# One transformer layer on one core: who places low parts and weights in the first chunk, and the last rows stored in blocks of 128 tokens

## The chip, the cores and the metric

The kernel runs on 1 core of one Trainium2 chip. The metric is the device time of one execution in microseconds (us). The kernel before took 2363.05 us, the median of 3 runs (2362.56 to 2366.21).

## What is computed

The reference is one layer: a layer norm of the input, an attention block and a feed-forward block that both read the normed input, and their sum added to the input. Cut to what matters:

```
xn = layernorm(x)                                  # x: 2 x 1024 x 1024, float32
q, k, v = bitnet(xn, Wq), bitnet(xn, Wk), bitnet(xn, Wv)   # 32 query heads, 8 key/value heads of 32
attn = softmax(q k^T / sqrt(32)) v
x + bitnet(attn, Wo) + ffn(xn)                     # ffn: gate and up 1024 -> 3584, down 3584 -> 1024, 4-bit weights

bitnet(x, W): s = max(mean(|W|, axis=1), 1e-8)
              y = (x @ sign(W)^T) * (s * scale)    # nan_to_num afterwards
```

So a projection needs two things of every weight tile: its signs, turned so that the input channel lies on the partitions, and the mean of its magnitudes, one number for each output channel.

## The kernel before

All 2048 tokens are taken in four chunks of 512 (`c` from 0 to 3), a chunk being four tiles of 128 tokens (`i`). The program goes: normalise and project the four chunks to q, k and v; attention over 32 units, with the first score rows woven into the last projections; the output projection; the feed-forward block over two halves of the tokens, gate and up first, then down; at the end of each half the sums are turned back to token rows and stored. There is no scheduler: every engine runs a list written out by hand, in order, and waits on named semaphores.

What happens ahead of the first projection and in chunk 0 (lines are those of the profile):

- VectorE takes the moments of the four first x tiles (L953, L954), normalises them (L987, L991), and ScalarE writes the float16 high part of each tile (`high`, L708). VectorE writes the low part, the remainder (`low`, L997). TensorE turns both, eight 128x128 transposes a tile (`turn_high` L1392, `turn_low` L1400). High parts go to PSUM bank 6 (tiles 0, 2) or 2 (tiles 1, 3), low parts to the bank after it, so a bank must be emptied before the tile after next can be turned. ScalarE copies both into `xT` (`evac_high` L678, `evac_low` L683).
- Twelve weight tiles of 128x1024 are loaded by SyncE's queue (L341) into eight places; tiles 8 to 11 wait until place 0 to 3 has been read for its signs and its magnitudes. For each tile ScalarE takes the signs (`signs`, L690, two buffers), TensorE turns them (`turn_weights`, L1384, PSUM banks 4 and 5), and somebody copies the result into `wT`: VectorE for the odd tiles from 3 on (`place_weights`, L1015), ScalarE for the others (`evac_weights`, L696). VectorE reduces each tile to its magnitudes (`magnitude`, L948). After all twelve it works out the channel scales `cc` (`cm_ok` is counted up when they stand), GpSimd takes a maximum over partitions (L591), and VectorE works out the three factors `fac` (`fac_ok`, L1055).
- TensorE's chunk is twelve projections of 16 matmuls 128x512 (`project`, L1439), p from 0 to 11, the two value tiles first. Between those of chunk 0 it turns the weights that later ones need: tiles 2 and 3 after p = 0, 4 and 5 after p = 1, 6 and 7 after p = 2, 8 after p = 3, 9 after p = 4, 10 after p = 6, 11 after p = 8. After p = 4 it turns the two value outputs (`turn_values`, L1453), and from p = 6 on it turns the x tiles of the next chunk; the first of these, `turn_high(4)`, writes bank 6 and so waits until the turned values there have been copied.
- Each projection is emptied and scaled by ScalarE (`evac_output`, L746, counts `y_ok`), which also writes a mask (`mask_output`, L753, one buffer); VectorE clamps and mends the output (`guard_output`, L1077 and L1081, counts `r_ok`), ScalarE writes its float16 head (L759) and VectorE its tail (L1094). Between these VectorE takes moments and normalises the next chunk, and in chunk 0 it places the turned values (`place_values`, L1087). The outputs of p = 0 to 3 stand in banks 0 to 3; p = 4 writes bank 0 again and so needs `y_ok` of p = 0.

At the end of the program, for the second half of the tokens, the last visits of `pe_down` (L1655) are scaled by ScalarE (L922) and VectorE (L1347), in two pairs of bank groups (`s2` 0: banks 0 to 3, `s2` 1: banks 4 to 7). Then `pe_turn` (L1671) turns four groups of 4 x 4 blocks, VectorE adds the input rows (`dve_turn`, L1355, 16 instructions of 128x512), and SyncE stores each group with one transfer of 1 MB (`store_rows`, L504). The first turn waits until every visit has been scaled.

```
            for k in (2, 4):
                evac_weights(k)
                signs(k + 2)
                signs(k + 3)
...
            act.wait_ge(s["fac_ok"], 1)
            for c in range(NC):
```

This is ScalarE's list just ahead of its first `evac_output`: the wait for the factors stands in front of all outputs, and tiles 6 and up are placed behind the first of them.

## Time and profile before

| what | value |
|---|---|
| median of the runs | 2363.05 us |
| the profiled execution's own time | 2364.19 us |
| its span, first to last instruction | 2362.1 us |
| TensorE busy (matmul) | 2305.1 us, 98% of the span |
| VectorE, ScalarE, GpSimd busy | 76%, 67%, 41% |
| TensorE's mean granted clock | 0.995 of full |

Busy time counts an engine's compute instructions alone. The span is cut in the page into 40 slices; TensorE is at 9 tenths or more in all of them but the first (6 tenths) and the last (8 tenths). The chain of work that ended last is TensorE's from about 1089 us on, broken by a few pieces of VectorE, and VectorE's at the very end.

### The profile page before, as it was taken

The page shows a single profiled execution, that of the slowest core. Times are in us where ns is not written, and L with a number is a line of the kernel's source. Part 1 is how long each engine was busy: PE and PEld are TensorE (multiplying, and loading weights), DVE is VectorE, ACT ScalarE, POOL GpSimd, SP SyncE. Part 2 cuts the span into 40 slices and gives each one's busy share as a digit, 9 for nine tenths or more (in the row PEclk, how much of TensorE's full clock was granted, in tenths as well). Part 3 has the DMA queues.
Part 4 walks back from the last instruction along what each step waited for, and adds up shares of the span by engine and source line. Part 5 has one row for each costly group of instructions (what it writes and reads, how often), then busy time and mean ns, then how long its engine had stood idle before and what let it go on. Part 6 is the DMA issues. An engine that isn't in the chain of part 4 may idle for free.

```text
span 2362.1 us, 45029 instructions
## 1 busy us (share of the span) xinstructions
PE 2305.1 (98%) x18561; PEld 1020.5 (43%) x18561; DVE 1802.5 (76%) x2314; ACT 1581.5 (67%) x2050; POOL 967.6 (41%) x531
## 2 busy tenths in 40 slices
PE   6999999999999999999999999999999999999998
PEld 3443344444444444434444444444444444444444
DVE  7878888888888888846577777777777777777777
ACT  5774788888888888872266666666665666666664
POOL 0000599999999999980022222210002222221000
PEclk9999999999999999999999999999999999999999
DMA  5130466555666655663211111131124111114111
GB/s 184 36 100 5 82 92 97 90 92 89 91 90 99 91 90 90 88 116 112 90 36 36 36 36 36 52 110 36 36 72 143 36 36 36 36 50 182 36 36 72
DMA packets 179905, 175.52 MB, mean 74 GB/s; under 512 B 87586, under 2 KB 127394, under 8 KB 179702
## 3 DMA queue, kind: packets, MB, share of 16 engines
q1 hardware_dynamic: 117430, 150.62, 20.5%
q0 software_dynamic: 62272, 22.03, 12.3%
q8 instruction: 147, 2.41, 0.4%
q14 instruction: 56, 0.46, 0.1%
HBM read 160.08 MB, written 65.45 MB: 95 GB/s over the span
## 4 chain that ended last, share of the span: by engine, by line
PE 53%; DVE 1%; issue 0%; ACT 0%; DVEq 0%
PE ps L1639 33%; PE ps L1655 16%; PE ps L1610 4%; PE ps L1671 0%; DVE zone L1355 0%; DVE xT L1355 0%; PE ps L1523 0%; DVE sm L1248 0%; ACT zone L922 0%; DVE zone L1065 0%; DVE zone L1066 0%; DVE zone L1259 0%; DVEq L140 0%; ACT zone L862 0%; DVE zone L1069 0%
## 5 line engine op out<-in xcount | busy, mean ns | idle before, releaser
L1639 PE MATMUL ps<-xT,zone 128*128 128x512 f16 x3584 | 774.6, 379 | 2.7 <-DVE zone L1355 2.7
L1103 DVE TENSOR_REDUCE zone<-ps 128x1 f32<-128x512 f32 x1024 | 639.2, 683 | 142.0 <-PE ps L1414 138.1
L779 ACT ACTIVATE zone<-ps,sm 128x512 f32<-128x512 f32 x1024 | 623.9, 698 | 144.8 <-PE ps L1464 144.2
L605 POOL TENSOR_TENSOR zone<-zone 128x1024 f32<-128x1024 f32 x252 | 643.9, 2687 | 135.8 <-ACT zone L779 102.8
L1332 DVE TENSOR_SCALAR ps<-ps,zone_c 128x1024 f32<-128x1024 f32 x392 | 506.7, 1293 | 160.8 <-PE ps L1639 158.7
L903 ACT ACTIVATE ps<-ps,zone_c 128x1024 f32<-128x1024 f32 x392 | 426.6, 1088 | 259.9 <-PE ps L1639 259.9
L1639 PEld LDWEIGHTS ps<-xT,zone 128*128 128x128 f16 x3584 | 350.2, 98 | 426.3 <-DVE zone L1355 4.2
L1464 PE MATMUL ps<-zone 98*32 98x512 f16 x4096 | 408.4, 380 | 4.2 <-ACT zone L779 3.8
L1414 PE MATMUL ps<-zone 96*32 96x512 f16 x4096 | 407.5, 381 | 4.5 <-issue 2.5
L1655 PE MATMUL ps<-zone 128*128 128x512 f16 x1792 | 387.1, 379 | 0.0
L1343 DVE TENSOR_SCALAR ps<-ps,zone_c 128x1024 f32<-128x1024 f32 x216 | 279.2, 1293 | 93.1 <-PE ps L1655 92.9
L651 POOL CAST zone<-zone 128x1024 f16<-128x1024 f32 x56 | 58.1, 1037 | 703.5 <-DVE zone L1336 703.5
L917 ACT ACTIVATE ps<-ps,zone_c 128x1024 f32<-128x1024 f32 x216 | 235.1, 1088 | 137.8 <-PE ps L1655 137.8
L1478 PE MATMUL ps<-zone 128*32 128x512 f32 x2048 | 268.6, 595 | 2.6 <-ACT zone L779 0.7
L1655 PEld LDWEIGHTS ps<-zone 128*128 128x128 f16 x1792 | 175.4, 98 | 211.4
L1464 PEld LDWEIGHTS ps<-zone 98*32 98x32 f16 x4096 | 117.7, 96 | 180.4 <-ACT zone L779 80.8
L1414 PEld LDWEIGHTS ps<-zone 96*32 96x32 f16 x4096 | 115.3, 96 | 180.1 <-DVE zone L1103 76.9
L1439 PE MATMUL ps<-xT,zone 128*128 128x512 f16 x768 | 180.3, 390 | 3.0 <-ACT xT L683 3.0
L659 POOL TENSOR_TENSOR xT<-xT,zone 128x1024 f32<-128x1024 f32 x8 | 18.7, 2355 | 361.8 <-ACT zone L922 361.8
L1493 PE MATMUL ps<-zone 128*32 128x512 f32 x1024 | 133.2, 592 | 0.4 <-DVE zone_c L1114 0.4
L653 POOL TENSOR_TENSOR zone<-zone 128x1024 f16<-128x1024 f32 x56 | 119.1, 2127 | 4.5
L1439 PEld LDWEIGHTS ps<-xT,zone 128*128 128x128 f16 x768 | 74.1, 100 | 97.7 <-issue 21.5
(137 smaller groups left out, 1331.5 us busy)
## 6 DMA issues: line engine op xcount, KB each, us to landing
zone<-dequantised SPq DMA_DIRECT2D x84, 512.0 KB, 3.6
dequantised<-zero_points SPq DMA_DIRECT2D x84, 256.0 KB, 4.3
zone<-zone SPq DMA_DIRECT2D x384, 32.0 KB, 2.4
zone<-_attn_hidden_states_dram SPq DMA_DIRECT2D x16, 512.0 KB, 6.4
zone<-inverse_sums SPq DMA_DIRECT2D x128, 64.0 KB, 2.5
attention<-zone SPq DMA_DIRECT2D x32, 256.0 KB, 2.0
xT<-attention SPq DMA_DIRECT2D x4, 2048.0 KB, 12.0
dequantised<-in_L_ffn_gate_w_dram POOLq DMA_DIRECT2D x28, 256.0 KB, 6.3
```

The costliest lines, as they stand in the source:

```text
L605: nc.gpsimd.tensor_tensor(duo[n % 3], prob[:, prob_slot(e), :], prob[:, prob_slot(e + 2), :], add).then_inc(s["sum_ok"], 1)
L779: A(prob[:, prob_slot(e), m % 2 * 512:(m % 2 + 1) * 512], ps[:, 3 + m % 3, :], ACT.Exp, scale=gam[:, 0:1]).then_inc(s["exp_ok"], 1)
L903: A(pair, pair, ACT.Copy, scale=tab[:, t, 0, g:g + 1]).then_inc(s["act_ok"], 1)
L1103: V.tensor_reduce(mxs[:, u % 2, half, i % 16:i % 16 + 1], ps[:, (2 * i + half) % 3, :], AX, amax).then_inc(s["max_ok"], 1)
L1332: V.tensor_scalar(pair, pair, tab[:, t, 1, g:g + 1], None, mult).then_inc(s["dve_ok"], 1)
L1343: V.tensor_scalar(pair, pair, dtab[:, it, o:o + 1], None, mult).then_inc(s["dve_ok"], 1)
L1414: last = MM(ps[32 * a:32 * a + 32, c % 3, :], qst[u % 3][0:96, i % 16 // 4, c0:c0 + 32], kst[0:96, u // 2 % 2, half * 512:(half + 1) * 512 ...
L1439: last = MM(ps[:, output_bank(n), :], wT[:, kt, f * P:(f + 1) * P], xT[:, b2, part, kt, s2 * 512:(s2 + 1) * 512], start=(kt == 0 and part ...
L1464: last = MM(ps[32 * b:32 * b + 32, 3 + m % 3, :], kst[0:98, u // 2 % 2, kt * P + 32 * b:kt * P + 32 * b + 32], qst[u % 3][0:98, 2 * hp + a ...
L1478: last = MM(ps[32 * h:32 * h + 32, 6, :], vst[:, u // 2 % 2, kt, :], prob[:, prob_slot(2 * kt + h // 2), h % 2 * 512:(h % 2 + 1) * 512], s ...
L1639: last = MM(ps[:, 4 * s2 + 2 * m + c, :], ring[:, buf, m * H + g * P:m * H + (g + 1) * P], xT[:, hf, part, g, c * 512:(c + 1) * 512], star ...
L1655: last = MM(ps[:, 4 * s2 + 2 * m + c, :], ring[:, k % RING, (it % 4) * 512 + o * P:(it % 4) * 512 + (o + 1) * P], hT[:, it, part, c * 512: ...
```

## The change

Four parts.

1. Low parts. VectorE copies the low parts of tiles 0, 1 and 3 of chunk 0 out of PSUM (`place_low`), two of them before and after its own `low(3)`; ScalarE keeps that of tile 2. The waits follow through a new semaphore, `xlv_out`.
2. Weights and magnitudes. VectorE reduces all twelve weight tiles in one run. ScalarE places tiles 2 to 6 (VectorE keeps 7, 9, 11), each behind the signs of the tile two further on, and takes the signs of tiles 8 and 9 ahead of its first `evac_output`. That output now waits for `cm_ok` in place of `fac_ok`.
3. First values. The turned values of chunk 0 are placed by ScalarE like those of the other chunks (`evac_turned_values(0)`, at p = 4), and `place_values` goes. On ScalarE `high(4)` moves from p = 4 to p = 3 and `high(5)` from p = 5 to p = 4.
4. Last rows. Each of the last four groups is stored by four transfers of 256 KB, one for each VectorE instruction, and the first of the last turns no longer waits for the very last visit.

```diff
@@ wait_weights and by_dve
-            return k % 2 == 1 and k >= 3
+            return k % 2 == 1 and k >= 7
@@ new, on PE in turn_low, project and turn_values
+        def wait_low_parts(engine, n):
+            engine.wait_ge(s["xlv_out"], min(n, 2) if n < 4 else 3)
+            if n >= 3:
+                engine.wait_ge(s["xl_out"], 1 if n < 5 else n - 3)
@@ SyncE
+            def store_blocks(n):
+                for b in range(4):
+                    sp.wait_ge(s["turn_ok"], 4 * (4 + n) + b + 1)
+                    sp.dma_start(rows_of(out, 1, n)[:, b, :], rows(1, n)[:, b, :]).then_inc(s["out_ok"], 16)
...
-                store_rows(1, n)
-            sp.wait_ge(s["out_ok"], 16 * 8)
+                store_blocks(n)
+            sp.wait_ge(s["out_ok"], 16 * (4 + 16))
@@ ScalarE, ahead of the outputs
             evac_high(1)
             high(3)
-            evac_low(0)
-            evac_low(1)
             evac_high(2)
+            evac_high(3)
             evac_low(2)
-            evac_high(3)
-            evac_low(3)
             signs(2)
             signs(3)
-            for k in (2, 4):
+            for k in range(2, 7):
+                signs(k + 2)
                 evac_weights(k)
-                signs(k + 2)
-                signs(k + 3)
+            signs(9)
...
-            act.wait_ge(s["fac_ok"], 1)
+            act.wait_ge(s["cm_ok"], 1)
@@ ScalarE, chunk 0
-                        if p == 0:
-                            evac_weights(6)
-                            signs(8)
-                            signs(9)
-                        elif p == 3:
+                        if p == 3:
                             evac_weights(8)
                             signs(10)
                         elif p == 4:
                             signs(11)
+                            act.wait_ge(s["fac_ok"], 1)
+                            evac_turned_values(0)
                         elif p == 7:
                             evac_weights(10)
                     mask_output(c, p)
+                    if c == 0 and p == 3:
+                        act.wait_ge(s["fac_ok"], 1)
+                        high(i)
...
-                            high(i)
-                        elif p == 5:
+                            high(i if c else i + 1)
+                        elif p == 5 and c:
                             high(i + 1)
@@ VectorE
-            for i in range(4):
+            for i in range(3):
                 low(i)
-            for k in range(3):
+            place_low(0)
+            low(3)
+            place_low(1)
+            place_low(3)
+            for k in range(NW):
                 magnitude(k)
...
-            for k in range(3, 5):
-                magnitude(k)
-            place_weights(3)
-            for k in range(5, 8):
-                magnitude(k)
-            place_weights(5)
-            for k in range(8, 12):
-                magnitude(k)
...
-                    if c == 0 and p == 4:
-                        place_values()
@@ PE
-                            pe.wait_ge(s["v_out" if c else "v0_out"], 2 * c if c else 2)
+                            pe.wait_ge(s["v_out"], 2 * c + 2)
...
-                pe_turn(1, n, n % 2, HALVES * HALF_VISITS)
+                pe_turn(1, n, n % 2, HALVES * HALF_VISITS - (n == 0))
```

VectorE's list from the low parts to the magnitudes. Before (the first rows are `low` on tiles 0, 1 and on 2, 3; TENSOR_REDUCE is `magnitude`; COPY is `place_weights(3)` and `(5)`):

```order
L997 SCALAR_TENSOR_TENSOR zone<-zone,sm 128x1024 [waits h_ok] x2
L997 SCALAR_TENSOR_TENSOR zone<-zone,sm 128x1024 [waits xl_pe,h_ok] x2
L948 TENSOR_REDUCE sm<-zone 128x1 [waits w_in0]
...
L948 TENSOR_REDUCE sm<-zone 128x1 [waits w_in4]
L1015 COPY zone<-ps 128x8x128 [waits wT_pe]
L948 TENSOR_REDUCE sm<-zone 128x1 [waits w_in5]
```

And with the change (COPY to `xT` is `place_low`, of tile 0, then of tiles 1 and 3):

```order
L1006 SCALAR_TENSOR_TENSOR zone<-zone,sm 128x1024 [waits h_ok] x2
L1006 SCALAR_TENSOR_TENSOR zone<-zone,sm 128x1024 [waits xl_pe,h_ok]
L1018 COPY xT<-ps 128x8x128 [waits xl_pe]
L1006 SCALAR_TENSOR_TENSOR zone<-zone,sm 128x1024 [waits xl_pe,h_ok]
L1018 COPY xT<-ps 128x8x128 [waits xl_pe] x2
L957 TENSOR_REDUCE sm<-zone 128x1 [waits w_in0]
L957 TENSOR_REDUCE sm<-zone 128x1 [waits w_in1]
```

Three copies came in ahead of the magnitudes, and the two copies of weight tiles that stood among them are gone.

ScalarE's list around the first output. Before (zone<-zone 128x1024 is `signs`, zone<-ps 128x8x128 is `evac_weights`, zone<-ps,sm 128x512 is `evac_output`):

```order
L690 ACTIVATE zone<-zone 128x1024 [waits wT_pe,w_in6]
L690 ACTIVATE zone<-zone 128x1024 [waits wT_pe,w_in7]
L746 ACTIVATE zone<-ps,sm 128x512 [waits qkv_pe,fac_ok]
L696 ACTIVATE zone<-ps 128x8x128 [waits wT_pe]
L690 ACTIVATE zone<-zone 128x1024 [waits wT_pe,w_in0]
L690 ACTIVATE zone<-zone 128x1024 [waits wT_pe,w_in1]
L753 ACTIVATE zone_c<-zone 128x512 [waits y_ok]
```

And with the change:

```order
L701 ACTIVATE zone<-zone 128x1024 [waits wT_pe,w_in7]
L707 ACTIVATE zone<-ps 128x8x128 [waits wT_pe]
L701 ACTIVATE zone<-zone 128x1024 [waits wT_pe,w_in0]
L707 ACTIVATE zone<-ps 128x8x128 [waits wT_pe]
L701 ACTIVATE zone<-zone 128x1024 [waits wT_pe,w_in1]
L754 ACTIVATE zone<-ps,sm 128x512 [waits qkv_pe,cm_ok]
L761 ACTIVATE zone_c<-zone 128x512 [waits y_ok]
```

The first output stood ahead of weight tile 6 and of the signs of tiles 8 and 9, and stands behind them now.

## Rows read from the trace of the kernel before

**Rows 1.** The page, busy time of each engine over the span.

```profile
PE 2305.1 (98%) x18561; PEld 1020.5 (43%) x18561; DVE 1802.5 (76%) x2314; ACT 1581.5 (67%) x2050; POOL 967.6 (41%) x531
```

**Rows 2.** Timeline of TensorE, start and duration in us, with idle and releaser.

```profile
25.38 0.61 PE L1400 MATMUL ps<-id,zone 128*128 128x128 f16 x8 [0.31 <-ACT xT L683]
29.04 6.14 PE L1439 MATMUL ps<-xT,zone 128*128 128x512 f16 x16 [3.05 <-ACT xT L683]
...
35.91 3.62 PE L1439 MATMUL ps<-xT,zone 128*128 128x512 f16 x16
...
44.60 3.62 PE L1439 MATMUL ps<-xT,zone 128*128 128x512 f16 x16
50.76 0.62 PE L1384 MATMUL ps<-id,zone 128*128 128x128 f16 x8 [2.54 <-ACT zone L690]
51.21 5.30 PE L1439 MATMUL ps<-xT,zone 128*128 128x512 f16 x16
...
58.15 7.07 PE L1439 MATMUL ps<-xT,zone 128*128 128x512 f16 x32
...
69.43 1.04 PE L1392 MATMUL ps<-id,zone 128*128 128x128 f16 x8 [3.76 <-DVE zone L1087]
70.26 6.04 PE L1439 MATMUL ps<-xT,zone 128*128 128x512 f16 x16
```

**Rows 3.** Busy time by stretch: PE, PEld, DVE, ACT, POOL; then clock, DMA, GB/s.

```profile
29.00:36.00 7.00, 6.96 (x33) 3.17 (x34) 1.43 (x2) 2.12 (x3) 0.00 (x0) 0.63 0.87 264
...
66.00:77.00 11.00, 7.57 (x40) 3.92 (x41) 10.32 (x16) 9.56 (x14) 0.00 (x0) 0.69 0.60 191
77.00:108.00 31.00, 31.00 (x186) 15.85 (x184) 22.62 (x46) 22.14 (x33) 0.00 (x0) 1.00 0.01 1
```

**Rows 4.** Timeline of VectorE, 23 to 63 us.

```profile
23.51 1.28 DVE L997 SCALAR_TENSOR_TENSOR zone<-zone,sm 128x1024 f16<-128x1024 f32 x1 [0.73 <-PE ps L1400]
...
24.71 5.72 DVE L948 TENSOR_REDUCE sm<-zone 128x1 f32<-128x1024 f32 x5
...
45.76 0.17 DVE L1031 TENSOR_SCALAR sm<-sm 128x12 f32<-128x12 f32 x1
...
48.03 0.68 DVE L1015 COPY zone<-ps 128x1024 f16<-128x1024 f16 x1
...
52.25 0.75 DVE L1081 COPY_PREDICATED zone<-zone_c,zone 128x512 f32<-128x512 int32 x1 [0.84 <-ACT zone_c L753]
...
56.84 0.77 DVE L1081 COPY_PREDICATED zone<-zone_c,zone 128x512 f32<-128x512 int32 x1
...
61.69 0.73 DVE L1081 COPY_PREDICATED zone<-zone_c,zone 128x512 f32<-128x512 int32 x1
```

**Rows 5.** Groups of ScalarE by line and shape, 29 to 90 us: busy, mean ns; idle.

```profile
L690 ACT ACTIVATE zone<-zone 128x1024 f16<-128x1024 f32 x10 | 10.1, 1060 | 0.0
L746 ACT ACTIVATE zone<-ps,sm 128x512 f32<-128x512 f32 x11 | 7.5, 680 | 6.7 <-DVE sm L1055 5.2 <-PE ps L1439 1.5
...
L696 ACT ACTIVATE zone<-ps 128x1024 f16<-128x1024 f16 x5 | 5.1, 1019 | 6.3 <-PE ps L1384 6.3
```

**Rows 6.** Timeline of the end, all engines.

```profile
2344.34 1.28 DVE L1347 SCALAR_TENSOR_TENSOR xT<-ps,zone_c,xT 128x1024 f32<-128x1024 f32 x1 [0.44 <-PE ps L1655]
...
2345.72 5.54 PE L1671 MATMUL ps<-id,xT 128*128 128x128 f32 x48 [1.42 <-issue]
2346.46 10.62 DVE L1355 SCALAR_TENSOR_TENSOR xT<-ps,sm,xT 128x512 f32<-128x512 f32 x16 [0.84 <-PE ps L1671]
2349.21 8.27 SPq L504 DMA_DIRECT2D out_dram<-xT  x4
```

**Rows 7.** Source of the row stores L504: time from issue to landing.

```profile
DMA to landing us min/median/max: 4.2/4.3/4.5
```

**Rows 8.** Source of the 256 KB attention stores L489: time from issue to landing.

```profile
DMA to landing us min/median/max: 2.0/2.0/5.2
```

**Rows 9.** DMA queues, 2349 to 2362 us: GB/s in 40 slices.

```profile
GB/s 0 0 0 208 365 391 391 391 384 365 372 321 403 391 384 403 384 372 359 328 397 410 365 397 397 365 391 321 397 391 391 378 397 359 384 397 378 177 0 0
```

35 lines of the change are left out of this document (18 added, 17 removed).

## The prediction, made before the change was run

> **What bounds the kernel now.** I read the page first. TensorE is busy 98% of the span [rows 1], so a change pays only where TensorE stands still, where it runs at the lower clock, or behind its last matmul. The page's slices put both places at the two ends, and the change touches just these. Next comes TensorE's own timeline of chunk 0 [rows 2]. The reader is to see three stalls with their releasers: 3.05 us ahead of the first projection (ScalarE's low parts), 2.54 us ahead of weight tile 8 (ScalarE's signs), 3.76 us ahead of `turn_high(4)` (VectorE's `place_values`). Behind each stall the next 16 matmuls take 6.14, 5.30 and 6.04 us, where the undisturbed ones take 3.62. The stretches show why: the granted clock is 0.63 in 29 to 36 us and 0.69 in 66 to 77 us, so part of each ran at the lower of the two levels, 1.2 GHz, and from 77 us on TensorE is full at clock 1.00 [rows 3]. So chunk 0 is the last place where the other engines hold it up for long. Then I read the lists of VectorE and ScalarE in that stretch [rows 4, 5] for what they do while TensorE waits, and the end of the timeline with the DMA views [rows 6 to 9].
>
> Consecutive instructions overlap by about 0.1 us on both engines: five magnitudes fill 5.72 us [rows 4], a step of 1.13. By the same overlap a sign costs ScalarE about 0.95, a weight copy 0.91, an output 0.6 [rows 5].
>
> **Part 1, low parts.** Before, ScalarE copied all eight tiles, the last of them just ahead of 29.04. Now VectorE ends `low(3)` at 24.79 as before (23.51 + 1.28) [rows 4], places tile 1 by 25.4 (a copy of this shape takes 0.68 [rows 4]), TensorE turns the low part of tile 3 at 25.5 where it did at 25.38 (0.61 [rows 2]), and VectorE places that by 26.8. ScalarE's share behind its last `high` is three copies where it was six, 2.7 us less, so it is no longer last. The first projection starts at 26.9, not 29.04: **2.1 us**. What is queued behind the new copies is the run of magnitudes, costed next. The stall is shorter and the matmuls are dense earlier, so the clock should rise earlier within the projection: I take 5.1 us for it where it took 6.14, **1.0 us** (bounds: 0, and 2.5 where it runs as the undisturbed one of 3.62). Sum 3.1: the second projection starts at 32.8, not 35.91 [rows 2].
>
> **Part 2, weights and magnitudes.** The next three projections go at 4.35 us each, turns of weights included (35.91 to 44.60 in two [rows 2]). Ahead of the first output ScalarE owes two signs and two copies in such a period, 2 x 0.95 + 2 x 0.91 = 3.7 us, so it keeps up, and the fourth projection ends at 32.8 + 2 x 4.35 + 3.6 = 45.1. VectorE's magnitudes start at 26.7, and 12 x 1.13 brings them to 40.3. Before they ended at 45.7, when the scales began [rows 4]. So `cm_ok` stands at 41.6. ScalarE is through with the signs of tile 9 at about 44.1, so the first output is there at 44.8. TensorE wants it at 45.4, for the fifth projection. So the stall of 2.54 goes, and so does the slow stretch behind it: the fifth projection starts at 45.4, not 51.21, and takes 3.6, not 5.30. **Gain so far 7.3.** The cover here is thin, 0.6 us; if ScalarE is later by more, TensorE waits for it one to one.
>
> What is late next: the second value output must have passed VectorE before `turn_values` ends. VectorE needs 9.6 us from `place_weights(7)` to there (48.03 to 57.61 [rows 4]), of which 0.84 waited for a mask that ScalarE now writes earlier. From the factors at 42.6 that is 51.2. TensorE is there at 49.7: a wait of 1.5 where there was nearly none. The sixth projection starts at 51.7, not 58.15: gain 6.4.
>
> **Part 3, first values.** Two projections and one turn take 7.4 us (58.15 to 65.67 [rows 2]): TensorE is at `turn_high(4)` at 59.1. ScalarE now empties the values behind: the third output through VectorE at 55.9 (4.8 after the second, as 57.61 to 62.42 [rows 4]), then a mask 0.5, `high(4)` 1.0, a head 0.6, an output 0.7, signs 0.95, and the two copies 1.25: 61.0. TensorE waits 2.0 instead of 3.76 and resumes at 61.1, not 69.43: gain 8.3. A slow stretch may follow (6.04 before; I take 4.9). VectorE's `low(4)` is through at about 67.7, one microsecond behind TensorE, and two copies of high parts are 0.4 late each. I take 0.8 to 1.9 off for these: **the head gives 7.5** when TensorE's full stretch is reached. After that the same work follows, full, and nothing there is tied to absolute time. The three loads of SyncE that now wait for later magnitudes (weight tiles 9 to 11, one for each 1.13 us) are read 8 us after their issue and cost nothing. Bounds: 4.5, if the clock gives nothing back and ScalarE is 1 us late, and 9.
>
> The Trainium skill (TensorE: Matmul & The Clock Gate, the part on the clock gate) says that the number of slow matmuls at a start varies between runs of one kernel. One profile can't show that; it is a reason to expect some scatter.
>
> **Part 4, last rows.** The first turn waited for VectorE's last scaling (to 2345.62) and now comes right behind the last matmul, at 2344.3. Its transposes are done before VectorE is free, so VectorE starts its 16 adds at 2345.6, not 2346.46 [rows 6]: 0.84. They fill 10.62 without a gap and end at 2356.2. The stores: four of 1 MB at intervals of 2.64 us, each landing after 4.3 [rows 6, 7], the last at 2361.6; the pipe moves the 4.19 MB (16 x 256 KB) at some 385 GB/s all the time [rows 9], 10.9 us. Now the first 256 KB leaves at 2346.4 in place of 2349.21. By the pipe the end is 2346.4 + 0.9 (before it moved data 0.9 after the issue) + 10.9 = 2358.2. By the last add it is 2356.2 + 2.0, for the nearest row of that size, the attention stores [rows 8], = 2358.2. **3.1 us**, taking 0.3 off because both limits meet. Bounds: 0.8, if smaller transfers move slower by as much as they start earlier, and 3.6.
>
> The attention stores of 256 KB land in 2.0 us in the trace [rows 8]. The Trainium skill (DMA: Bandwidth & Descriptors, Anatomy of one DMA) gives about 2.0 us fixed plus the bytes at 436 GB/s, by a fit for the other path of issue, and its rules for kernel authors ask for 1 MiB or more in one DMA. By its sum the last store would land 2.6 us after its add, and part 4 would give 2.5.
>
> **Sum.** 7.5 + 3.1 = 10.6 us against the profiled execution's own 2364.19: 2353.6 us. That execution is 1.1 us above the median of the runs. Three slow stretches make up 6.6 us of its chunk 0, so a median run may have had one less; the changed kernel has fewer of them to lose, and I keep 2353.6.
>
> **Rivals.**
>
> *The helpers become the bound in chunk 0.* For it: VectorE is busy 10.32 of 11 us and ScalarE 9.56 in 66 to 77 [rows 3], and the change moves two value copies and two weight copies onto ScalarE. Then the waits after p = 4 grow and the clock falls again: the head gives about 4, the time is 2364.2 - 4 - 3.1 = 2357. Against it: ScalarE idles 6.7 us ahead of its outputs and 6.3 ahead of weight copies [rows 5], nearly all before 48.2 us, and there it gets most of its new work.
>
> *The stores gain nothing but the earlier adds,* since the pipe is full already [rows 9] and each transfer adds a little: 2364.2 - 7.5 - 0.8 = 2355.9.
>
> *What chunk 0 gives is lost later,* in waits of the attention stage that were covered: 2361. Against it, TensorE is full for 31 us behind chunk 0 [rows 3] and 98% over all [rows 1].
>
> *Slower: the queue runs one store at a time.* If each 256 KB store held SyncE's queue for its 2.0 us [rows 8], 16 would take 32 us from 2346.4 and end at 2378.4, 16.8 later than now; less the head's 7.5, the time would be 2373.5. It decides from about 1.4 us a store. By the page's sum of 2.6 us each it would be 41.6 us. Against it: four stores land after 4.3 each and are issued 2.64 apart [rows 6, 7], so two are in flight together, and the rate never drops between them.
>
> **How the numbers follow.** Forecast 0.74, helpers 0.12, stores 0.06, lost later 0.05, one at a time 0.03. The range takes in the first three and the bounds of the clock's part: 2350.5 to 2358.2. A measurement of this kernel can tell some 0.2% from no change, 4.7 us, so faster means below 2358.3. Faster: all of the first and third case and most of the second, 0.90. Same: the fourth and the rest, 0.07. Slower: 0.03.
>
> **What would show it.** First projection at about 26.9; no stall ahead of weight tile 8 and no slow stretch in the fifth projection; stalls of about 1.5 at the second `turn_values` (released by VectorE) and 2 at `turn_high(4)` (by ScalarE's value copies); the second chunk's first projection 7 to 8 us earlier; 16 stores 0.66 apart, the last landing about 2 us after the last add. Wrong if the first output comes after TensorE wants it, if the clock stays at 1.2 GHz through the fifth projection, or if the last store lands over 4 us after its add.

## The result, and the profile after

| | median of the runs | lowest to highest | ratio to the kernel before (95% interval) |
|---|---|---|---|
| changed kernel, first comparison | 2353.12 us (5 runs) | 2351.58 to 2358.72 | 0.9957 (0.9944 to 0.9971) |
| changed kernel, second comparison (e9 below) | 2355.84 us (8 runs) | 2353.08 to 2358.99 | 0.9974 (0.9964 to 0.9984) |

The kernel before took 2366.21 us in the first comparison (5 runs) and 2361.94 us in the second (13 runs). The ratio is not taken from the two medians, so it need not be their quotient. As time the ratios are gains of 10.1 us (6.9 to 13.3) and 6.1 us (3.8 to 8.5). The predicted 2353.6 us is met; the predicted gain of 10.6 us lies within the first interval and above the second. The stages below tell what of it the change earned. A stage is a stretch of TensorE's own timeline: the head up to the last projection of chunk 0, the middle, and the end behind the last matmul of `pe_down`.

The profiled execution of the changed kernel took 2351.58 us, span 2349.7, against 2364.19 and 2362.1 before. Where the 12.4 us between the two spans lie:

| stage | before | after | gain | predicted |
|---|---|---|---|---|
| head: to the start of the last projection of chunk 0 | 90.15 | 83.26 | 6.9 | 7.5 |
| middle: from there to the end of the last matmul of `pe_down` | 2254.1 | 2250.8 | 3.4 | 0 |
| end: from there to the end of the span | 17.8 | 15.7 | 2.1 | 3.1 |

Of the page's busy times [rows 1] only TensorE's moved, by 7.5 us; 6.6 us of that are the three slow stretches of chunk 0, which are gone:

```profile
PE 2297.6 (98%) x18561; PEld 1019.1 (43%) x18561; DVE 1802.8 (77%) x2313; ACT 1581.5 (67%) x2051; POOL 966.9 (41%) x531
```

TensorE's timeline of chunk 0 in the changed kernel, to be laid beside [rows 2] (L1439 is a projection, L1384 `turn_weights`, L1456 `turn_values`, L1392 `turn_high`, L1400 `turn_low`):

```profile
27.28 3.61 PE L1439 MATMUL ps<-xT,zone 128*128 128x512 f16 x16 [0.99 <-DVE xT L1018]
...
31.62 3.62 PE L1439 MATMUL ps<-xT,zone 128*128 128x512 f16 x16
...
44.22 3.62 PE L1439 MATMUL ps<-xT,zone 128*128 128x512 f16 x16
...
51.80 0.66 PE L1456 MATMUL ps<-id,zone 128*128 128x128 f32 x4 [3.08 <-DVE zone L1090]
52.29 7.07 PE L1439 MATMUL ps<-xT,zone 128*128 128x512 f16 x32
...
61.63 0.62 PE L1392 MATMUL ps<-id,zone 128*128 128x128 f16 x8 [1.82 <-ACT zone L774]
62.09 3.62 PE L1439 MATMUL ps<-xT,zone 128*128 128x512 f16 x16
...
68.34 0.62 PE L1400 MATMUL ps<-id,zone 128*128 128x128 f16 x8 [2.64 <-DVE zone L1006]
...
83.26 15.92 PE L1439 MATMUL ps<-xT,zone 128*128 128x512 f16 x73
```

The first projection starts 1.76 us earlier and takes 3.61 us where it took 6.14, so the second starts 4.3 earlier. The stall of 2.54 ahead of weight tile 8 is gone, and the fifth projection starts at 44.22 instead of 51.21: 7.0 us ahead. The lead is 5.9 us at the sixth projection, 8.2 at the eighth (62.09 for 70.26) and 6.9 at the last one of chunk 0, so behind the fifth nothing is won that lasts. Three stalls follow, 3.08, 1.82 and 2.64 us, in place of the one of 3.76. The same stretches as in [rows 3] show the clock (columns: stretch, length, then PE, PEld, DVE, ACT, POOL busy; granted clock, DMA share, GB/s):

```profile
29.00:36.00 7.00, 7.00 (x58) 4.17 (x57) 7.00 (x8) 4.05 (x5) 0.00 (x0) 1.00 0.88 296
...
66.00:72.00 6.00, 3.65 (x29) 2.18 (x30) 5.74 (x9) 5.91 (x9) 0.00 (x0) 1.00 0.44 145
```

The granted clock is 1.00, 2.4 GHz, in both. Between 66 and 72 us TensorE has work for 3.65 us of the 6, while VectorE is busy 5.74 and ScalarE 5.91: the helpers hold it up. VectorE's timeline, beside [rows 4], shows why the stall of 3.08 exists: the magnitudes are one run of 13.60 us from 26.94 on, and the mended outputs (COPY_PREDICATED) end at 51.75 and 56.59.

```profile
26.94 13.60 DVE L957 TENSOR_REDUCE sm<-zone 128x1 f32<-128x1024 f32 x12
...
51.02 0.73 DVE L1090 COPY_PREDICATED zone<-zone_c,zone 128x512 f32<-128x512 int32 x1
...
55.84 0.75 DVE L1090 COPY_PREDICATED zone<-zone_c,zone 128x512 f32<-128x512 int32 x1
...
67.01 1.27 DVE L1006 SCALAR_TENSOR_TENSOR zone<-zone,sm 128x1024 f16<-128x1024 f32 x1
```

The end, all engines, beside [rows 6]:

```profile
2333.86 3.66 PE L1674 MATMUL ps<-id,xT 128*128 128x128 f32 x32
2334.07 1.28 DVE L1347 SCALAR_TENSOR_TENSOR xT<-ps,zone_c,xT 128x1024 f32<-128x1024 f32 x1 [0.44 <-PE ps L1658]
2335.27 10.62 DVE L1355 SCALAR_TENSOR_TENSOR xT<-ps,sm,xT 128x512 f32<-128x512 f32 x16
...
2336.04 10.45 SPq L515 DMA_DIRECT2D out_dram<-xT  x16
```

The turn starts with the end of the last matmul and VectorE adds without the wait of 0.84, as predicted. The source of the new stores L515 (16 of 256 KB; duration of the issue in ns) and, in the next line, their landing (the time from the issue until the store is reported complete), beside [rows 7]:

```profile
L515 SPq DMA_DIRECT2D out_dram<-xT x16: 332/416/855, 2336.0 to 2345.9; - x16
...
DMA to landing us min/median/max: 2.4/2.8/3.5
```

The last store is issued at 2345.9 with the last add and lands 3.4 us later, not 2.0. The DMA queues from 2334 to 2350 us, GB/s in 40 slices, beside [rows 9]:

```profile
GB/s 0 0 0 0 0 41 0 276 338 31 312 389 394 364 389 389 379 374 379 389 374 404 364 384 394 364 389 369 379 394 364 384 379 399 374 358 31 0 0 0
```

The start has a hole (31 between 338 and 312). VectorE isn't its cause: the second store was issued as soon as its add was done, at 2336.70, but the issue took 855 ns. Another transfer lies there, which the view of these queues lists as `q8 instruction`, 16 KB: it began at 2336.30 (the slice with 41) and took 0.9 us of one of the 16 DMA engines. From the twelfth slice on the pipe is as full as before, and it is last. The section on the stores comes back to this transfer.

### The profile page after: what moved, and what is told of

The parts are those of the page before. It is cut to its first block, busy times and chain, and to the rows that moved or that the text cites. A ratio compares the mean times of both kernels' runs of the same rounds, so it can differ in the third digit from the quotient of the medians.

```text
span 2349.7 us, 45046 instructions
## 1 busy us (share of the span) xinstructions
PE 2297.6 (98%) x18561; PEld 1019.1 (43%) x18561; DVE 1802.8 (77%) x2313; ACT 1581.5 (67%) x2051; POOL 966.9 (41%) x531
## 4 chain that ended last, share of the span: by engine, by line
PE 90%; DVE 5%; ACT 3%; issue 1%; DMA 0%; SPq 0%; POOL 0%; DVEq 0%; ACTq 0%
PE ps L1642 33%; PE ps L1658 16%; PE ps L1414 10%; PE ps L1467 9%; PE ps L1481 9%; PE ps L1496 5%; PE ps L1613 4%; PE ps L1439 3%; DVE sm L957 1%; ACT zone L787 1%; ACT zone L719 0%; DVE zone L996 0%; ACT zone L767 0%; DVE zone L1090 0%; ACT zone L754 0%
## 5 line engine op out<-in xcount | busy, mean ns | idle before, releaser
L1642 PEld LDWEIGHTS ps<-xT,zone 128*128 128x128 f16 x3584 | 350.3, 98 | 426.2 <-DVE zone L1355 4.2
L1658 PE MATMUL ps<-zone 128*128 128x512 f16 x1792 | 387.1, 379 | 0.0
L1439 PE MATMUL ps<-xT,zone 128*128 128x512 f16 x768 | 173.7, 379 | 1.0 <-DVE xT L1018 1.0
L670 POOL TENSOR_TENSOR xT<-xT,zone 128x1024 f32<-128x1024 f32 x8 | 18.7, 2362 | 361.8 <-ACT zone L931 361.8
L1613 PE MATMUL ps<-zone 128*128 128x512 f16 x512 | 112.3, 379 | 1.2 <-DVE zone L1259 1.1
```

The costliest lines, as they stand in the source:

```text
L1642: last = MM(ps[:, 4 * s2 + 2 * m + c, :], ring[:, buf, m * H + g * P:m * H + (g + 1) * P], xT[:, hf, part, g, c * 512:(c + 1) * 512], star ...
L1658: last = MM(ps[:, 4 * s2 + 2 * m + c, :], ring[:, k % RING, (it % 4) * 512 + o * P:(it % 4) * 512 + (o + 1) * P], hT[:, it, part, c * 512: ...
```

## The experiments

Twelve kernels ran, each with profiled and timed runs beside the kernel before. One table for all; the start of the second chunk, of which the expectations speak, is 3.45 us behind the last projection of chunk 0 in every trace.

| kernel | first projection | last projection of chunk 0 | last matmul of `pe_down` ends | end stage | median (runs) | ratio (95%) |
|---|---|---|---|---|---|---|
| before | 29.04 | 90.15 | 2344.30 | 17.8 | | |
| changed | 27.28 | 83.26 | 2334.03 | 15.7 | 2353.12 (5) | 0.9957 (0.9944 to 0.9971) |
| e9 changed again | 27.29 | 83.94 | 2338.39 | 16.3 | 2355.84 (8) | 0.9974 (0.9964 to 0.9984) |
| e1 end only | 28.80 | 87.89 | 2341.68 | 15.9 | 2360.23 (10) | 0.9993 (0.9983 to 1.0003) |
| e2 head only | 27.25 | 83.74 | 2336.01 | 17.8 | 2356.87 (7) | 0.9975 (0.9964 to 0.9985) |
| e5 part 1 undone | 28.97 | 86.27 | 2346.31 | 16.1 | 2357.80 (10) | 0.9979 (0.9968 to 0.9990) |
| e6 part 3 undone | 26.79 | 82.73 | 2336.48 | 16.3 | 2355.21 (5) | 0.9968 (0.9955 to 0.9981) |
| e7 output ahead of weights | 27.21 | 83.86 | 2345.06 | 15.7 | 2357.76 (10) | 0.9983 (0.9973 to 0.9993) |
| e3 stores of 1 MB | 27.26 | 83.19 | 2334.78 | 16.8 | 2355.73 (7) | 0.9969 (0.9958 to 0.9981) |
| e4 1 MB x3, then 256 KB x4 | 27.25 | 83.17 | 2335.08 | 17.9 | 2355.79 (6) | 0.9969 (0.9958 to 0.9981) |
| e10 stores of 512 KB | 28.53 | 84.47 | 2337.59 | 16.4 | 2355.45 (6) | 0.9967 (0.9955 to 0.9979) |
| e8 values, low(4) earlier | 28.57 | 83.52 | 2335.01 | 15.9 | 2352.44 (4) | 0.9959 (0.9944 to 0.9974) |
| e11 no mask in chunk 0 | 27.76 | 77.24 | 2335.89 | 15.8 | 2351.99 (4) | 0.9951 (0.9937 to 0.9965) |
| e12 mask by GpSimd | 27.04 | 88.80 | 2343.29 | 15.7 | 2361.84 (12) | 0.9998 (0.9986 to 1.0009) |

The kernel before had a median of 2361.89 us (23 runs) beside e1, e2, e5 and e6, 2362.50 (18) beside e7, e3, e4 and e8, 2361.94 (13) beside e9, e10 and e11, and 2362.33 (17) beside e12.

### The end alone, and the head alone (e1, e2)

e1 is the kernel before with part 4; e2 is the changed kernel without it:

```diff
# e2, against the changed kernel
-                store_blocks(n)
-            sp.wait_ge(s["out_ok"], 16 * (4 + 16))
+                store_rows(1, n)
+            sp.wait_ge(s["out_ok"], 16 * 8)
...
-                pe_turn(1, n, n % 2, HALVES * HALF_VISITS - (n == 0))
+                pe_turn(1, n, n % 2, HALVES * HALF_VISITS)
```

> The kernel before with part 4 alone. My theory: the stage behind the last matmul shrinks as in the changed kernel, from 17.8 us (last down matmul to the end of the span) to 15.7, and nothing else moves: the second chunk's first projection stays at 91 to 94 us, and the time is 2.1 us below before. Rival (the small stores owe their gain to the clock or to chance of that run): 17 or more, time within 1 us of before.

> The changed kernel with part 4 undone (1 MB stores, first turn behind the last visit). My theory: the second chunk's first projection at 86.1 to 87.1 us as in the changed kernel, the end stage 17.8 us, the time 7 to 10 us below before and about 2 above the changed kernel. Rival (the head's gain is not its own but comes of one execution without slow stretches of the clock): the time within 5 us of before.

e1: the end stage went from 17.8 to 15.9 us, and the median from 2361.89 to 2360.23, 1.7 less, with an interval that takes in no change. e2: 5.0 us less in the median, 3.5 to 8.5 by the ratio, for 7 to 10 expected. The two medians add up to 6.7 us, the two ratios to 7.6, each with some 2.4 us either way. What TensorE's timeline of e1, whose head is the old one, shows:

```profile
28.80 5.27 PE L1445 MATMUL ps<-xT,zone 128*128 128x512 f16 x16 [2.96 <-ACT xT L689]
...
49.65 1.03 PE L1390 MATMUL ps<-id,zone 128*128 128x128 f16 x8 [2.53 <-ACT zone L696]
50.47 4.71 PE L1445 MATMUL ps<-xT,zone 128*128 128x512 f16 x16
...
68.26 0.62 PE L1398 MATMUL ps<-id,zone 128*128 128x128 f16 x8 [3.76 <-DVE zone L1093]
68.72 3.62 PE L1445 MATMUL ps<-xT,zone 128*128 128x512 f16 x16
```

The stalls are those of [rows 2] to a tenth, but the clock is kinder: 5.27, 4.71 and 3.62 us for the three projections that took 6.14, 5.30 and 6.04. The three are 3.9 us shorter together and the first starts 0.2 earlier, yet the last projection of chunk 0 comes only 2.3 earlier (87.89 for 90.15): TensorE then waits for VectorE and ScalarE in places where it didn't before (0.23, 0.31 and 0.26 us). So the old head takes 87.9 or 90.2 us, mostly by the clock. The new one takes 82.7 to 84.5 over seven traces of it (changed, e9, e2, e3, e4, e10) or with part 3 undone (e6). The head is worth 4 to 7 us (3.4 where e10's inputs came late), according to which two executions are compared.

### Part 1: low parts back to ScalarE (e5)

```diff
             evac_high(1)
             high(3)
+            evac_low(0)
+            evac_low(1)
             evac_high(2)
-            evac_high(3)
             evac_low(2)
+            evac_high(3)
+            evac_low(3)
@@ VectorE
-            for i in range(3):
+            for i in range(4):
                 low(i)
-            place_low(0)
-            low(3)
-            place_low(1)
-            place_low(3)
```

> Part 1 undone in the changed kernel: ScalarE copies all eight tiles of chunk 0 again. My theory: the first projection starts at 29.0 instead of 27.3 us, with a slow stretch behind it (the first projection takes 5 to 6 us), and the second chunk starts at 87.6 to 88.7 instead of 86.7; time 1 to 3 us above the changed kernel. Rival (VectorE and ScalarE, by their whole work in chunk 0, set when the second chunk starts, and the first projection's start does not matter): 86.7 to 87.2, the same time.

TensorE's timeline of e5:

```profile
28.97 6.28 PE L1436 MATMUL ps<-xT,zone 128*128 128x512 f16 x16 [3.05 <-ACT xT L692]
...
54.10 0.66 PE L1453 MATMUL ps<-id,zone 128*128 128x128 f32 x4 [1.01 <-DVE zone L1087]
...
70.64 0.62 PE L1397 MATMUL ps<-id,zone 128*128 128x128 f16 x8 [2.63 <-DVE zone L1007]
```

The old stall of 3.05 is back, with a slow projection of 6.28 us behind it, and the last projection of chunk 0 starts at 86.27, 3.0 later (expected for the second chunk: 87.6 to 88.7; measured 89.7). The second projection is 4.4 us late, but the stall at `turn_values` is 1.01 instead of 3.08, and behind it TensorE is 2.3 late: almost half of the delay is absorbed by a stall in which TensorE would have waited for VectorE anyway. The further 0.7 is a slow stretch at the ninth projection, which e9 has with the whole change.

The second `turn_values` also tells what the parts are worth there. It starts at 51.80 in the changed kernel, 54.10 with part 1 undone, 56.50 in e1 and 57.66 before. So part 1 is worth 2.3 us at that point, and part 2 another 2.4 (against e1) to 3.6 (against before). Of part 2 only the order around the first output was undone by itself (e7); that the run of magnitudes, freed of the two weight copies, makes up the rest is not shown by a run.

### Part 3: first values back to VectorE (e6)

```diff
@@ ScalarE
                         elif p == 4:
                             signs(11)
-                            act.wait_ge(s["fac_ok"], 1)
-                            evac_turned_values(0)
...
-                            high(i if c else i + 1)
+                            high(i)
@@ VectorE
+                    if c == 0 and p == 4:
+                        place_values()
```

> Part 3 undone in the changed kernel: VectorE places the first values, high(4) and high(5) back in their old places. By the stall alone (my prediction's way of counting) TensorE resumes at turn_high(4) 2 us later, the eighth projection (p = 7) starts at about 64 instead of 62.1, and all behind it is 2 us later: second chunk at 88.7, time 2 us above the changed kernel. Rival (the helpers' total work bounds chunk 0): the stall at turn_high(4) grows by 2 us, but the later one of 2.6 us at turn_low(4) shrinks by as much, and the second chunk starts at 86.5 to 87.3, the same time.

TensorE's timeline of e6:

```profile
51.31 0.65 PE L1463 MATMUL ps<-id,zone 128*128 128x128 f32 x4 [1.39 <-DVE zone L1088]
...
63.09 0.62 PE L1399 MATMUL ps<-id,zone 128*128 128x128 f16 x8 [3.77 <-DVE zone L1094]
63.55 5.30 PE L1446 MATMUL ps<-xT,zone 128*128 128x512 f16 x16
```

The stall at `turn_high(4)` is 3.77 us again, as before the change, instead of 1.82; it even brings a slow projection of 5.30. But the stall at `turn_low(4)`, 2.64 in the changed kernel, is gone, and the last projection of chunk 0 starts at 82.73, half a microsecond *earlier* than with part 3. Moving the value copies to ScalarE moved the wait from one place to the next; the head gained nothing by it. (Its first projection was itself 0.5 us earlier: from first to last projection both take 56.0 us to within 0.1, so it is a tie.)

### Half of part 2: the first output ahead of tile 6 (e7)

```diff
-            for k in range(2, 7):
+            for k in range(2, 6):
                 signs(k + 2)
                 evac_weights(k)
-            signs(9)
...
-            act.wait_ge(s["cm_ok"], 1)
+            act.wait_ge(s["fac_ok"], 1)
...
-                        if p == 3:
+                        if p == 0:
+                            evac_weights(6)
+                            signs(8)
+                            signs(9)
+                        elif p == 3:
```

> Half of part 2 undone in the changed kernel: ScalarE's first output waits for the factors again and stands ahead of weight tile 6 and of the signs of tiles 8 and 9. My theory: TensorE waits about 2 us for the signs of tile 8 ahead of the fifth projection (start 46 to 46.5 instead of 44.2), the wait of 3.1 at the second turned values shrinks to 2, and the second chunk starts at 87.0 to 87.7 instead of 86.7: time 0.5 to 1.5 above the changed kernel. Rival (one to one): 88.7 and 2 us.

TensorE's timeline of e7:

```profile
45.57 0.62 PE L1387 MATMUL ps<-id,zone 128*128 128x128 f16 x8 [1.71 <-ACT zone L701]
...
52.42 0.66 PE L1459 MATMUL ps<-id,zone 128*128 128x128 f32 x4 [1.88 <-DVE zone L1093]
```

A stall of 1.71 for ScalarE's signs is back, the fifth projection starts 1.8 later, and the stall at `turn_values` shrinks from 3.08 to 1.88. The last projection of chunk 0 starts at 83.86 (so the second chunk at 87.3; 87.0 to 87.7 expected), inside what two executions of the changed kernel gave (83.26 and 83.94). Against the first of them, which like e7 has no slow projection, the order around the first output is worth 0.6 us. e7's median is higher than its head explains; its profiled execution lost time in the middle, told below.

### The stores: 1 MB, 512 KB, and small ones behind large ones (e3, e10, e4)

```diff
# e3: stores of 1 MB, the early first turn kept
-                store_blocks(n)
-            sp.wait_ge(s["out_ok"], 16 * (4 + 16))
+                store_rows(1, n)
+            sp.wait_ge(s["out_ok"], 16 * 8)
# e10: pairs of blocks
-                for b in range(4):
-                    sp.wait_ge(s["turn_ok"], 4 * (4 + n) + b + 1)
-                    sp.dma_start(rows_of(out, 1, n)[:, b, :], ...
+                for b in (0, 2):
+                    sp.wait_ge(s["turn_ok"], 4 * (4 + n) + b + 2)
+                    sp.dma_start(rows_of(out, 1, n)[:, b:b + 2, :], ...
# e4: only the last group in blocks
-            for n in range(4):
-                store_blocks(n)
+            for n in range(3):
+                store_rows(1, n)
+            store_blocks(3)
```

> The changed kernel with 1 MB stores: of part 4 only the earlier first turn is left. If each store lands 4.3 us after its issue, the end stage is 0.9 shorter than before: 16.8 us, with the last add 3.9 to 5 ahead of the end as before; time 1.1 above the changed kernel. If the pipe's rate set the end, the same 16.8 would come out, but the landings would be over 4.5.

> The changed kernel with the last rows stored by 512 KB (eight stores). By the pipe's rate with its holes: with 1 MB stores all data took 11.2 us from the first packet to the last, with 256 KB 12.0 to 12.7, with holes near the start. Halves start 0.66 us later than quarters, and if holes come with the number of transfers the data takes about 11.4: end stage 15.6 to 15.9 us, the same as or a little below the quarters. Rival (the landing of the last store sets it: 3.0 to 3.3 for 512 KB behind the last add instead of 2.8): 16.2 or more.

> The changed kernel with three stores of 1 MB and only the fourth group in four of 256 KB. If the landing time of the last small store sets the end (2.0 us by the prediction's row), the end stage is 15.7 us or less, as with 16 small ones. If the pipe's rate does (385 GB/s from the first store on), it has started 2 us later and ends later: 16.2 to 16.8 us.

e3's end stage is 16.8 us, as expected: the early turn gives 0.9, and smaller stores the rest, down to 15.7 to 16.3 over the nine traces that have all of part 4. e10 took 16.4, not the 15.6 to 15.9 expected. e4 took 17.9, all that the early turn had given and more; neither theory expected it (15.7, or 16.2 to 16.8). Its four small stores L515 at the source, the landing of its three 1 MB stores L509, and its DMA queues from 2338 to 2353 us:

```profile
L515 SPq DMA_DIRECT2D out_dram<-xT x4: 539/1187/1213, 2345.0 to 2348.1; - x4
...
DMA to landing us min/median/max: 4.9/5.8/6.0
```

```profile
GB/s 0 0 0 0 0 317 344 377 355 377 360 371 339 399 393 399 366 388 360 371 371 426 366 410 366 366 415 361 404 382 366 415 361 404 224 27 27 22 0 0
```

The issues of the small stores took 1187 ns in the median, where they took 416 in the changed kernel, so the last one left SyncE at 2349.3, some 2.4 us behind the last add. The last slices, 27, 27 and 22 GB/s where the full pipe has some 385, are about what one of the 16 engines moves (24): one has packets left when the others are through.

It is tempting to blame the mixture of small stores with large ones, but the first 1 MB store already landed 6.0 us behind its issue, at 2345.05, where e3's took 4.3; the first small store was issued only at 2344.99. What differs before that is the transfer `q8 instruction` met above. In e4 it began at 2340.1, inside the first store (DMA queues, 2339 to 2342 us), and 3.2% of 16 engines over 3 us are 1.5 us of one engine:

```profile
q8 instruction: 1, 0.02, 3.2%
```

In the traces of before, e2 and e3 it came ahead of the first store. In e10 it began at 2342.6, inside the second store, and took 1.4 us of one engine; the tail is of the same kind (35, 23 and 18 GB/s in the last slices from 2340 to 2354 us). The small stores show the same. e6, where it began at 2344.3, has the landings of its stores before it (source L516, issued from 2338 to 2342.5 us) and from it on (2344 to 2350):

```profile
DMA to landing us min/median/max: 2.0/2.1/2.2
...
DMA to landing us min/median/max: 2.6/3.1/3.9
```

One issue of 1146 ns stands right behind it; the nine traces with all of part 4 each have one such issue of 0.9 to 1.3 us there. Where the transfer came within 1 us of the first store the end stage was 15.7 to 16.1 us (seven traces), where it came in the middle of the row 16.3 (e9, e6). Without the last 1.3 us, in which few engines had packets, e4 would be at 16.7, within the 16.2 to 16.8 of the pipe's rate. So the 17.9 of e4 and the 16.4 of e10 are no verdict on mixed sizes or on 512 KB: like against like, e10's 16.4 stands beside 16.3 with 256 KB. All this is read from one trace of each kernel; no run moved the transfer by itself, and why the issues of small stores behind large ones stayed at 1.2 us isn't shown.

From first to last packet the 4.19 MB took 11.2 us in 1 MB stores (before, e2, e3) and 12.0 to 12.7 in stores of 256 KB (changed 12.0, e9 12.7). Full, the pipe takes 0.70 us for 256 KB and VectorE makes them in 0.66, so small stores have no slack in which a delayed engine could catch up.

### Who bounds chunk 0 now (e8, e11, e12)

e8 is the changed kernel with the value copies of ScalarE at p = 3 instead of 4 (and the signs of tile 11 behind them), and VectorE's `low(4)` at p = 5 instead of 6. e11 leaves out mask and mending of the twelve outputs of chunk 0, the work of `nan_to_num`; VectorE clamps the output in place and nothing else. e12 is e8 with the masks of chunk 0 made by GpSimd.

```diff
# e8
-                        elif p == 4:
-                            signs(11)
                             act.wait_ge(s["fac_ok"], 1)
                             evac_turned_values(0)
+                        elif p == 4:
+                            signs(11)
@@ VectorE
+                        if (c, p) == (0, 5):
+                            low(i)
# e11 and e12, ScalarE
-                    mask_output(c, p)
+                    if c:
+                        mask_output(c, p)
# e12, GpSimd
+            for p in range(12):
+                pool.wait_ge(s["y_ok"], p + 1)
+                if p >= 1:
+                    pool.wait_ge(s["r_ok"], p)
+                nc.gpsimd.tensor_tensor(mask, output(p), output(p), sub).then_inc(s["mask_ok"], 1)
```

> The changed kernel with two things moved in chunk 0: ScalarE places the first values at p = 3, ahead of the mask that waits for VectorE, and VectorE writes low(4) at p = 5 instead of p = 6. My theory: the stall at turn_high(4) (1.8 us) goes, the one at turn_low(4) (2.6 us) shrinks to under 1, but the helpers' work holds the second chunk: start at 85.2 to 85.9 instead of 86.7, time about 1 below the changed kernel. Rival (each stall counts in full): 83 and 3.5 us below.

> The changed kernel, in chunk 0 without the mask and the mending of the projections' outputs (ScalarE's mask_output and VectorE's predicated copy are left out, the clamp writes the output): the guard against values that aren't numbers is missing in that chunk. This takes 0.53 us x 12 from ScalarE and 0.63 us x 12 from VectorE. If the helpers' work bounds chunk 0, the second chunk's first projection starts at 79.5 to 81 us instead of 86.7, and the waits of TensorE behind the fifth projection shrink from 7.8 us to 3. Rival (the waits come of the order of the lists, not of the load): less than 3 us earlier, over 83.5.

> e8's order (first values and low(4) earlier) and, in chunk 0, the mask written by GpSimd as output minus output, so that ScalarE has 0.53 us x 12 less to do; nothing is left out. From the first projection's start to the second chunk's it was 59.4 to 60.1 us in five executions of the changed kernel's order or near it, 58.3 in e8, and 52.9 without mask and mending. If the helpers' load bounds chunk 0: 56.5 to 57.5, and the time 1.5 to 3 us below the changed kernel, 8 to 10 below before. Rival (GpSimd's instruction of 1.3 to 1.6 us comes too late for VectorE's mending, or slows VectorE): 58.5 or more, no gain over e8.

TensorE's timelines of e8 and of e11:

```profile
53.09 1.09 PE L1458 MATMUL ps<-id,zone 128*128 128x128 f32 x4 [3.08 <-DVE zone L1090]
...
68.93 0.61 PE L1394 MATMUL ps<-id,zone 128*128 128x128 f16 x8 [1.80 <-ACT xT L689]
```

```profile
50.56 0.66 PE L1460 MATMUL ps<-id,zone 128*128 128x128 f32 x4 [1.36 <-DVE zone L1088]
...
63.27 0.62 PE L1404 MATMUL ps<-id,zone 128*128 128x128 f16 x8 [0.80 <-DVE zone L1007]
...
77.24 17.43 PE L1443 MATMUL ps<-xT,zone 128*128 128x512 f16 x80
```

e11: with one instruction of ScalarE and one of VectorE less for each output, the stalls shrink to 1.36 and 0.80 and the last projection starts at 77.24, so the second chunk at 80.7 (expected 79.5 to 81). From first to last projection that is 49.5 us instead of 56.0. So the work of VectorE and ScalarE on the outputs bounds chunk 0 after the change. Leaving it out takes load off both and also shortens the way of each output, which e11 can't tell apart; the busy times of the changed kernel speak for the load. From 26.9 to 61.5 us VectorE works 32.8 of 34.6 us, and then, up to the last projection, it is ScalarE that is busy 20.43 of 21.30 (columns as above):

```profile
62.00:83.30 21.30, 18.09 (x134) 9.91 (x132) 16.20 (x23) 20.43 (x29) 0.00 (x0) 1.00 0.30 99
```

Not all of e11's 6.5 us reaches the time: its median is 3.9 us below e9's, measured beside it, and its middle took 2258.7 us, 4.2 more than e9's. One profile of each can't say whether that is the scatter told of below.

In e8 the stalls at `turn_high(4)` and `turn_low(4)` are gone, and one of 1.80 us at the next high part, released by ScalarE's copy, stands in their place. (Part of the first is covered by a slow stretch: the two projections ahead took 8.36 us for 7.07.) e8's inputs came some 1.3 us late in its profiled execution; from first to last projection it took 55.0 us, 1.0 less than the changed kernel. Its median of 2352.44 us is the lowest of any kernel that computes the whole layer, but its interval overlaps both of the changed kernel's, so no gain over it is shown.

e12 missed in the other direction: 61.8 us from first to last projection, where some 53 to 54 had been expected. VectorE's groups from 40 to 85 us in e12 (count | busy, mean ns | idle, releaser), then in the changed kernel (40 to 87):

```profile
L1013 DVE SCALAR_TENSOR_TENSOR zone<-zone,sm 128x1024 f16<-128x1024 f32 x4 | 6.7, 1675 | 0.0
...
L1097 DVE COPY_PREDICATED zone<-zone_c,zone 128x512 f32<-128x512 int32 x9 | 6.6, 736 | 4.9 <-POOL zone_c L608 3.9
...
L1093 DVE TENSOR_SCALAR zone<-zone 128x512 f32<-128x512 f32 x10 | 5.9, 586 | 0.6 <-ACT zone L760 0.6
```

```profile
L1006 DVE SCALAR_TENSOR_TENSOR zone<-zone,sm 128x1024 f16<-128x1024 f32 x4 | 5.1, 1276 | 0.0
...
L1086 DVE TENSOR_SCALAR zone<-zone 128x512 f32<-128x512 f32 x11 | 4.6, 421 | 4.0 <-ACT zone L754 4.0
```

VectorE waits 3.9 us for GpSimd's masks, and its own instructions are slower: the low part takes 1675 ns in the mean for 1276, the clamp 586 for 421. VectorE's timeline shows which: two of the four low parts (L1013) began while GpSimd worked, at 68.55 and 75.30, and took 2.08 and 2.06 us, the other two 1.28 and 1.29; a clamp that began at 65.87, inside GpSimd's mask of 65.47 to 66.85, took 1.27 us, where most take 0.41 to 0.43. The Trainium skill (SBUF — State Buffer, SBUF: two separate sides) says that of a VectorE instruction with two SBUF inputs and a GpSimd instruction that reads SBUF the first to start holds a port pair that both need for its whole length, and the other waits. The trace agrees for the low parts, which have two inputs and began second. Giving work to an idle engine isn't free when it holds up the busy one.

### The changed kernel again, and what scatters (e9)

> The changed kernel once more, beside its kernel before on one chip. Heads (start of the second chunk's first projection) of four executions of the new order lie within 86.5 to 87.1 us and those of the old at 91.4 and 93.6; the stage behind the last matmul is 15.7 to 16.4 against 17.8. If these two differences are all, the time is 4.8 to 6.9 + 1.4 to 2.1 = 6.2 to 9.0 us below before. Rival: the first comparison's 10.1 is right (something in the attention stage gains too): over 9.5.

e9's time was 6.1 us below before, at the lower edge of the 6.2 to 9.0 expected, and its second chunk started at 87.4 (86.5 to 87.1). Its profile has two of the three stalls of the changed kernel's:

```profile
51.79 0.66 PE L1456 MATMUL ps<-id,zone 128*128 128x128 f32 x4 [3.06 <-DVE zone L1090]
52.28 8.76 PE L1439 MATMUL ps<-xT,zone 128*128 128x512 f16 x32
...
61.60 0.62 PE L1392 MATMUL ps<-id,zone 128*128 128x128 f16 x8
...
68.31 0.62 PE L1400 MATMUL ps<-id,zone 128*128 128x128 f16 x8 [2.64 <-DVE zone L1006]
69.22 5.30 PE L1439 MATMUL ps<-xT,zone 128*128 128x512 f16 x16
```

In place of the stall of 1.82 the two projections ahead of it ran partly at the lower clock (8.76 us for 7.07, granted clock 0.80), and TensorE reached `turn_high(4)` at 61.60 for 61.63: the slow stretch cost nothing. The clock fell again behind `turn_low(4)` (5.30 us for 3.62), and this made the last projection of chunk 0 0.7 late. The middle, identical code in all of these kernels, took 3.6 us more than in the first profile (2254.4 against 2250.8), 2260.0 in e5, and 2261.2 in e7, where TensorE stood still for 2.7 us at one instruction of the attention stage with no releaser. In the kernel before it took 2254.1 and in e1, with the old head, 2253.8; nine of the twelve traces with the new head or nearly so have 2250.8 to 2254.5, e11 2258.7. So the 3.4 us by which the first comparison's profiles differ in the middle lie within the scatter. The nine also speak against the rival by which the gain of chunk 0 is lost later; the three long middles it can't exclude. I did not find what makes these gaps.

## Why the prediction came out as it did

**The time was right, the gain probably overstated, by up to 4 us.** Predicted 10.6; e1 and e2 together give 6.7, the second comparison 6.1 (at most 8.5), the first 10.1 (at least 6.9). The stages give 4 to 7 for the head and 1.4 to 2.1 for the end. That the time came out to half a microsecond is in part luck: the eight runs of the second comparison have their median at 2355.84, still inside the predicted range.

**Part 1: mechanism right, size too small.** The first projection came at 27.28 (26.9 said). The clock's part was 2.5 us in the profile, not 1.0: the lower level didn't show at all, the bound of 3.62 that I had set. In e2, e6 and e12 the same projection took 5.2 to 5.3, in the eight other traces with part 1 it took 3.61. So this term is 1 to 2.5 by the execution, but it doesn't reach the end of chunk 0: e2, with 5.20, waits 1.48 us at `turn_values` where the changed kernel waits 3.08, and both start the sixth projection at 52.3. e5 shows that part 1 carries 2.3 us there, and at most 3.0 of the final head.

**Part 2: what it said of the fifth projection held, of the wait behind it not.** The stall for the signs went, and no slow stretch followed; ScalarE had the first output at 43.6, TensorE wanted it at 44.2, a cover of 0.6 as said. But the wait at the second `turn_values` was 3.08, not 1.5. VectorE was ready at 51.75, within 0.6 of the 51.2 predicted; TensorE was there at 48.7, 1.0 earlier than said, for the clock's sake. (The prediction's own terms add up to 51.4, and 7.5 for its "gain so far 7.3"; neither slip matters.) The working had the cause (VectorE needs 9.6 us from there), but the earlier arrival was booked as a gain and is only a longer wait. e5 and e7 show the same from the other side: 4.4 and 1.8 us of delay ahead of that wait shorten it to 1.01 and 1.88.

**Part 3 failed.** The wait at `turn_high(4)` was 1.82, for 2.0 predicted, and released by ScalarE's value copies as said. But "I take 0.8 to 1.9 off for these" was too little: `low(4)` was a stall of 2.64, as VectorE ended it at 68.28 and not at 67.7, with TensorE there at 65.7, a microsecond earlier than said because its projection wasn't slow. Counted in the prediction's way, 1.9 came off 9.4 (8.3, and 1.1 for a less slow stretch); measured, 3.3 came off 10.2 (7.8, and 2.4). e6 undoes the part and loses nothing. So the rival "the helpers become the bound" is what happens in chunk 0, even though the head as a whole came near the forecast: 6.9 of 7.5 against the profiled execution, which had three slow projections. Against e1's old head, with kinder clocks, it is 4.6, close to that rival's 4. The prediction had raised just this doubt ("a median run may have had one less") and then kept the sum.

**Part 4: the term was mis-sized, 2.1 for 3.1.** The adds came 0.84 earlier, as said. The steps that failed are "the last add plus 2.0" and the pipe's 10.9. The first store left 2.0 us behind the last matmul instead of 4.9, a lead of 2.9; but the data then took 12.0 us for 11.2, and 2.9 - 0.8 = 2.1 is what came out. The landing of 2.0 [rows 8] holds also for stores in a row: e6's first seven landed in 2.0 to 2.2. It doesn't hold once an engine is behind: the changed kernel's sixteen took 2.4 to 3.5. The term of the pipe, 10.9 us, was worked out from a rate over stores of 1 MB, among which no other transfer fell; the same rows give 11.2 from first to last packet. By the fit of the Trainium skill (DMA: Bandwidth & Descriptors, Anatomy of one DMA), made for the other path of issue, the last store would land, by estimate, 2.6 us behind its issue; it was 3.4. The rival that smaller stores bring nothing (0.8) falls in the traces: e3 has 16.8 with 1 MB stores, for 15.7 to 16.3. The rival of one store at a time falls too: sixteen went within 12.0 us.

The sign of each stall was right, and so was its releaser, but for the one at `turn_low(4)`, booked as one microsecond and measured as 2.64; the sum took the gains at almost full length though each ended in a wait for the same two engines.

## What to carry to other kernels

When a stall is removed ahead of an engine that waits again soon, follow the *other* engines to the next meeting: the gain is what is left there, not the length of the stall, and of two edits ahead of one such meeting only one may pay. The clock makes old stalls dearer in some executions than in others, so a gain read against one profile needs a second profile of the kernel before. Smaller last stores start sooner, but they leave the pipe no slack: look in the trace for other transfers among them before a difference of a microsecond is put down to the size of the stores, and take a landing time from a row of stores, not from one alone.

## What was unexpected

- One 16 KB transfer of the queue `instruction`, 0.9 to 1.5 us on one of 16 DMA engines, goes with a tail of 0.4 to 1.3 us at the end of the last stores in every trace where it falls among them, and with none (0.1 us) in the three where it came before.
- The same code up to the first projection put it at 26.8 to 27.3 us in eight traces, at 27.8 in one (e11) and at 28.5 in two (e8, e10), where the inputs had come later. That shifts the whole head by as much as part 3 was to give.
- A slow stretch of the clock needn't cost anything. In e3 the clock was at its lower level in the whole stretch behind the stall at `turn_values`:

```profile
51.00:57.00 6.00, 5.24 (x15) 2.42 (x16) 5.69 (x13) 3.50 (x5) 0.00 (x0) 0.50 0.00 0
```

Two projections ran slow, and the stall at `turn_low(4)` was 1.67 us instead of 2.64. The last projection of chunk 0 started at 83.19, as in the changed kernel (83.26), since the helpers, VectorE and ScalarE, set the pace.
